# Attention kernel on one Trainium2 core: probabilities times values in three fp32r passes, and the keys' norm factor on GpSimd

## The reference

```python
q = (draft_hidden @ Wq.T).reshape(bsz, draft_len, H, HD)          # H 16, HD 128
q = _rms_norm(q, q_norm_w).transpose(0, 2, 1, 3)
kv_in = jnp.concatenate([context_hidden, draft_hidden], axis=1)   # 64 + 64 tokens
k = (kv_in @ Wk.T).reshape(bsz, total_len, KVH, HD)               # KVH 4
v = (kv_in @ Wv.T).reshape(bsz, total_len, KVH, HD).transpose(0, 2, 1, 3)
k = _rms_norm(k, k_norm_w).transpose(0, 2, 1, 3)
q = _rope(q, draft_position_ids)
k = _rope(k, full_position_ids)
scores = jnp.einsum('bhqd,bhkd->bhqk', q, k) * SCALE
probs = jax.nn.softmax(scores, axis=-1)
attn = jnp.einsum('bhqk,bhkd->bhqd', probs, v)
return attn.transpose(0, 2, 1, 3).reshape(bsz, draft_len, H * HD) @ Wo.T
```

## Time and profile before

| | |
|---|---|
| median of 3 runs | 1236.04 us (1235.15 to 1237.65) |
| span of the profiled execution | 1234.9 us |
| PE / DVE / ACT / POOL busy | 98% / 82% / 72% / 74% |
| granted TensorE clock, mean | 0.998 |
| time of the units | from 29 to about 970 us |
| expert phase | from about 970 to the end |

### The profile page before, as it was taken

The page is one execution under the profiler, slowest core; times in us unless marked ns, Lnnn a source line. Parts: engine busy times, 40 slices in busy tenths (PEclk is TensorE's granted clock), DMA queues, the critical chain, the costliest instruction groups (busy, mean ns, idle before and its releaser), DMA issues.

```text
span 1234.9 us, 31490 instructions
## 1 busy us (share of the span) xinstructions
PE 1210.5 (98%) x8781; PEld 1141.9 (92%) x8782; DVE 1008.0 (82%) x2992; ACT 885.3 (72%) x3754; POOL 919.6 (74%) x1124
## 2 busy tenths in 40 slices
PE   6899999999999999999999999999999999999998
PEld 3788999999999999999999999999999999999997
DVE  8788888888888888888888888888888677777443
ACT  7978777777777777777777777777777546666322
POOL 2678887888888888888888887888887425555654
PEclk9999999999999999999999999999999999999999
DMA  6634233322222322222333333322236536554574
GB/s 179 196 105 131 78 105 105 106 89 89 89 89 89 94 89 89 94 89 93 109 109 102 101 100 119 101 75 75 75 109 205 199 103 187 162 162 146 186 239 151
DMA packets 128792, 148.57 MB, mean 120 GB/s; under 512 B 13824, under 2 KB 108288, under 8 KB 127968
## 3 DMA queue, kind: packets, MB, share of 16 engines
q1 hardware_dynamic: 122256, 130.16, 34.8%
q0 software_dynamic: 6480, 17.77, 3.9%
HBM read 66.93 MB, written 80.76 MB: 120 GB/s over the span
## 4 chain that ended last, share of the span: by engine, by line
PE 95%; ACT 2%; DVE 2%; issue 1%; another core or an unknown queue 0%; DMA 0%; SPq 0%; DVEq 0%; ACTq 0%
PE b_kv L1711 14%; PE b_q L1697 14%; PE b_o L1795 13%; PE b_sc L1769 9%; PE b_aT L1784 9%; PE b_pT L1777 5%; PE b_qT L1758 4%; PE b_q L2031 3%; PE b_kv L2031 3%; PE b_q L1828 2%; PE b_kT L1754 2%; PE b_kT L1828 2%; PE b_aT L1946 1%; PE b_pT L2048 1%; PE b_aT L2048 1%; PE b_o L1747 1%
## 5 line engine op out<-in xcount | busy, mean ns | idle before, releaser
L1711 PE MATMUL b_kv<-w_group,kv_in_hi 128*128 128x256 f32 x992 | 205.5, 305 | 0.0
L747 POOL TENSOR_TENSOR qk_r<-qk_me,minus_half 128x6 f32<-128x6 f32 x128 | 173.7, 1357 | 10.1 <-POOL qk_me L745 0.2
L957 ACT ACTIVATE probs<-b_sc,neg_max 128x128 f32<-128x128 f32 x512 | 180.5, 373 | 0.1
L751 POOL TENSOR_TENSOR q_rot<-q_rot,q_sin 128x512 f32<-128x512 f32 x128 | 163.8, 1279 | 6.8 <-DVE q_sin L1273 1.9
L1711 PEld LDWEIGHTS b_kv<-w_group,kv_in_hi 128*128 128x128 f32 x992 | 161.8, 190 | 6.7 <-issue 0.4
L1697 PE MATMUL b_q<-w_group,kv_in_hi 128*128 128x512 f32 x496 | 164.9, 413 | 0.0
L951 ACT ACTIVATE pT<-b_pT 128x512 f32<-128x512 f32 x128 | 76.7, 599 | 102.9 <-PE b_pT L1777 100.9
L1795 PE MATMUL b_o<-wo_hi,aT_hi 128*128 128x256 f32 x480 | 143.5, 299 | 0.1
L1769 PE MATMUL b_sc<-kT,qT 128*128 128x128 f32 x1024 | 135.8, 275 | 6.2 <-ACT qT L946 4.2
L754 POOL TENSOR_TENSOR q_rot<-q_rot,qk_r 128x512 f32<-128x512 f32 x128 | 133.5, 1043 | 10.0
L1711 PE MATMUL b_kv<-w_group,kv_in_lo 128*128 128x256 f32 x496 | 139.6, 281 | 0.0
(11 more groups left out here) (309 smaller groups left out, 3949.2 us busy)
## 6 DMA issues: line engine op xcount, KB each, us to landing
xs_scratch<-zeros SPq DMA_DIRECT2D x34, 1032.0 KB, 6.2
s_in<-xs_scratch SPq DMA_DIRECT2D x71, 129.0 KB
yT_scratch<-yT SPq DMA_DIRECT2D x32, 256.0 KB
yS<-yT_scratch SPq DMA_DIRECT2D x32, 256.0 KB
routed<-ys_scratch SPq DMA_DIRECT2D x32, 256.0 KB, 3.6
w_hi_all<-w_scratch SPq DMA_DIRECT2D x3, 1536.0 KB, 14.0
x_in<-in_x SPq DMA_DIRECT2D x32, 128.0 KB, 2.3
ctx_raw<-in_ctxT SPq DMA_DIRECT2D x32, 128.0 KB, 2.6
```

The lines of the kernel that those rows point to most:

```text
L747: nc.gpsimd.tensor_tensor(qk_r[g % 2][:], qk_me[:], minus_half[:, 0:REP + NB], ALU.pow).then_inc(r_ready, 1)
L751: nc.gpsimd.tensor_tensor(q_rot[g % 2][:], q_rot[g % 2][:], q_sin[g % 2][:], ALU.add) \
L957: last = nc.scalar.activation(probs[:, j, :], b_sc[:, j * P:(j + 1) * P], ACT.Exp, bias=neg_max[g % 2][:, j:j + 1], accum_out=row_sum[g % ...
L1711: last = nc.tensor.matmul(b_kv[:, s * 2 * HD:(s + 1) * 2 * HD], kv_in[p][a][:, c, 2 * s:2 * s + 2, :], wkv_of(b, c)[:, g % KVH, :], start= ...
```

## The change

Seven things are edited; none changes what is computed beyond rounding.

1. `attend`: the values (`v_s`) and the transposed probabilities (`pT`) become high and low parts, and each of the two 256-column fp32 matmuls becomes three fp32r ones. The high parts are the ACT copies that were there; the low parts are two new DVE subtractions in each unit, `values_lo` (128x256) and `probs_lo` (128x512), both reading PSUM.
2. `turn_keys` on DVE no longer multiplies by the norm factor: four 128x128 operations become two of 128x256. POOL multiplies the sum by the factor in `key_sum`, one more 128x256 operation.
3. DVE's order: `turn_keys(n+1)` moves from behind `score_max(n)` to right behind `turn_queries(n+1)`; `values_lo(n+1)` and `probs_lo(n-1)` stand in front of `score_max(n)`.
4. The copy of kT moves from DVE to ACT, in front of the copy of qT.
5. ACT's order: the copy of the transposed probabilities comes right behind the copy of qT, the scaling of the first probability block moves from the next unit to right behind the high part of attention, in front of the squares of the queries.
6. PE's order: `probs_T(n-1)` stands in front of `scores(n)` rather than behind it and behind the small matmuls.
7. `below`, `ones`, `mask` and `seen`, the small counts of the ranks, become bfloat16. Buffers: `junk` goes (the squares are written, as fp32, to the buffers that the turn overwrites), `q_sin` and `k_sin` have one buffer in place of two, with a wait on POOL's sums.

```diff
             def key_sum(n, g):
                 need(pool, k_turned, n + 1)
-                nc.gpsimd.tensor_tensor(k_rot[g % 2][:], k_rot[g % 2][:], k_sin[g % 2][:], ALU.add) \
+                nc.gpsimd.tensor_tensor(k_rot[g % 2][:], k_rot[g % 2][:], k_sin[:], ALU.add) \
+                  .then_inc(rot_summed, 1)
+                need(pool, rot_summed, 2 * n + 2)
+                nc.gpsimd.tensor_tensor(k_rot[g % 2][:], k_rot[g % 2][:],
+                                        qk_r[g % 2][:, REP:REP + NB].unsqueeze(2).to_broadcast([P, NB, HD]), ALU.mult) \
                   .then_inc(k_ready, 1)
...
+            def keys_out(n, g):
+                need(act, kT_done, n + 1)
+                nc.scalar.activation(kT[:].rearrange("p b n -> p (b n)"), b_kT[:, 0:NB * P], ACT.Copy).then_inc(k_out, 1)
...
                     if not (end and g == 3):
                         key_squares(n + 1, g + 1)
+                        values_out(n + 1, g + 1)
...
                     if not (first and u == 0):
+                        if not (first and u == 1):
+                            keys_out(n, g)
                         queries_out(n, g)
-                    if not (end and g == 3):
-                        values_out(n + 1, g + 1)
                     if not (first and u == 0):
-                        normalize_first(n - 1, g - 1)
+                        probs_out(n - 1, g - 1)
...
-                    if not (first and u == 0):
-                        probs_out(n - 1, g - 1)
...
                     exponentials(n, g)
...
                         attended_hi(n - 1, g - 1)
+                    if not (end and g == 3):
+                        normalize_first(n, g)
                     if not (end and g >= 2):
                         query_squares(n + 2, g)
...
             def turn_keys(n, g, p):
 
-                need(dve, v_out, n + 1)
-                need(dve, r_ready, n + 1)
+                need(dve, v_hi, n + 1)
+                need(dve, rot_summed, 2 * n)
...
+            def values_lo(n, g):
+                kv = b_kv[:].rearrange("p (b w n) -> p b w n", b=NB, w=2)
+                hi, lo = v_s[g % KVH]
+                nc.vector.tensor_tensor(lo[:], kv[:, :, 1, :], hi[:].bitcast(F32), ALU.subtract).then_inc(v_lo, 1)
+
+            def probs_lo(n, g):
+                need(dve, pT_hi, n + 1)
+                nc.vector.tensor_tensor(pT[LO][:].rearrange("p b n -> p (b n)"), b_pT[:],
+                                        pT[HI][:].rearrange("p b n -> p (b n)").bitcast(F32), ALU.subtract).then_inc(pT_lo, 1)
...
                     if not (end and g == 3):
                         turn_queries(n + 1, g + 1, t + (g == 3), p1)
+                        turn_keys(n + 1, g + 1, p1)
...
+                    if not (end and g == 3):
+                        values_lo(n + 1, g + 1)
+                    if not (first and u == 0):
+                        probs_lo(n - 1, g - 1)
                     score_max(n, g)
...
-                    if not (end and g == 3):
-                        turn_keys(n + 1, g + 1, p1)
...
             def attend(n, g):
-                need(pe, v_out, n + 1)
-                need(pe, pT_out, n + 1)
+                need(pe, v_lo, n + 1)
+                need(pe, pT_lo, n + 1)
                 for s in range(NB):
-                    last = nc.tensor.matmul(b_aT[:, s * REP * S:(s + 1) * REP * S], v_s[g % KVH][:, s, :],
-                                            pT[:, s, :], start=True, stop=True)
+                    for a, b in PASSES:
+                        last = nc.tensor.matmul(b_aT[:, s * REP * S:(s + 1) * REP * S], v_s[g % KVH][a][:, s, :],
+                                                pT[b][:, s, :], start=((a, b) == PASSES[0]), stop=((a, b) == PASSES[-1]))
...
+                    if not (first and u < 1):
+                        probs_T(n - 1, g - 1)
                     scores(n, g)
...
-                    if not (first and u < 1):
-                        probs_T(n - 1, g - 1)
```

91 lines of the change are left out of this document (46 added, 45 removed).

## The result

The changed kernel takes **1388.7 us** (median of 4 runs, 1387.3 to 1389.0) against 1236.0 (1235.2 to 1237.7) for the kernel before: 1.123 times as long, 95% interval 1.121 to 1.124. Slower was forecast, but 1296 us and at most 1328. The sign and the chain held, the size did not. Its span is 1385.6 us at a granted clock of 0.997, so the clock explains nothing.

What follows compares the result with a forecast made beforehand. PE bounds the kernel before; DVE's in-order chain was to bound it after. A tile of 31.3 us for 29.29 gives 49 us over 24 tiles, plus 7 and 4: +60 on 1234.9, forecast 1296 us, range 1268 to 1328.

Steps and rivals of the forecast that it cites:

- The new chain: DVE with ACT's exponentials, one unit's first exponential to the next: 6.57 us for 5.29 before, plus work done once a tile.
- the 93 forecast: Sign on PE: its busy time from 500 to 600 us falls from 100 to about 93.
- the sum: The four units of a tile, 8.15, 7.46, 7.84 and 7.87 us, give 31.3 us for 29.29 before.
- SBUF-only terms: DVE operations priced from earlier rows: probabilities 0.65 us, x_n with the residual 0.75, normalized rows 0.54.
- may shrink by 0.6: DVE's weight piece split, 1.27 us for 440 columns, might shorten; 15 us in the lower half of the range.
- Without it the ACT path holds: 6.92.: Unit g 2 to 3 without a weight piece: ACT's path sets the length, 6.92 us instead of 7.84.
- the chain is longer: Rival, chance 0.13: fp32 squares on ACT take 0.09 us more each, 0.3 to 0.5 a unit; 1330 to 1350 us.
- What the change does on PE: `attend`: six fp32r passes take 0.69 us for 0.86, gaining 0.17 a unit, 22 us, lost while PE waits.
- PE stays the bound: Rival, chance 0.06: DVE's chain stays below PE's new unit of 7.08 us; the 22 us come in full, 1211 to 1216.
- The counts: Two bfloat16 matmuls of 8 columns a tile on PE: at most 7 us in all, taken as nothing.
- What it does on POOL: One more 128x256 multiply a unit, taken as 0.60 us, plus 0.08 for the wait, right ahead of PE's `heads_T`.
- POOL becomes the bound: Rival, chance 0.06: the multiply fills POOL's wait for ACT's squares; tile 29.1 to 30.0 us, near 1243 us.

Runs made afterwards that it cites:

- x15: Changed kernel with POOL's rotary tables cut, the two-element addition moved behind the maxima and the layer norm's x_n moved to the end of unit g 0: 1288.4 us, ratio 1.044.
- x10: Changed kernel with both low-part subtractions on DVE (values and probabilities) cut to one element, all six passes multiplying high parts: 1297.3 us, ratio 1.051.
- x1: Changed kernel with the turn of the keys on DVE put back behind the maximum of the scores: 1316.4 us, ratio 1.064.
- x5: Kernel before with only the three fp32r passes in `attend`, all on high parts, no low parts computed: 1232.3 us, ratio 0.996.
- x7: x5 with the subtraction for the weight piece moved from the end of unit g 2 to the end of g 3: 1228.1 us, ratio 0.995.
- x12: Kernel before with the bfloat16 counts alone: 1231.0 us, ratio 0.998.
- x16: Changed kernel with low-part subtractions cut to one element, and the keys' turn and two-element addition behind the maxima: 1283.4 us, ratio 1.041.

## Why the prediction was right in its sign and wrong in its size

- **"The new chain" held.** ACT starts its exponentials 0.76 to 0.78 us after the maximum starts, 0.09 or 0.10 after its end, in every unit of the tile shown; DVE waits for the exponentials 0.8 to 1.3 us in each. PE is 88% busy for the 93 forecast. x15 confirmed the sum, 30.9 us a tile for 30.6. x10 and x1 moved the time by about what stands in the chain (91 us for 93; 72 for 81), but that close agreement is luck: both also freed stalled operations and both ran into POOL's late sin table.
- **The step that failed is the pricing of its SBUF-only terms**: probabilities 0.65, x_n 0.40 (in the 0.75 for x_n with the residual), and the normalized rows, 0.54, whose two-element addition had no term. They were read where POOL did not stop them (x_n and the rows beside its power, the probabilities behind the last 0.23 us of a sum) and then used at new places, where POOL was at work. Measured they were 1.81 and 1.29 in two units of four (0.56 in the others), 0.92, and 0.48 + 1.25. The warning was in the earlier trace rows: the weight piece took 1.27 us for 440 columns where 384 took 0.65. The prediction saw it, took it into its lower half only ("may shrink by 0.6"), and didn't ask why. Another stands in the earlier trace rows: the multiply at 514.02 took 0.64 us, for the 0.56 it takes alone, because it began inside POOL's sum of 513.52. What was missed is worth some 90 us.
- **A smaller miss: "Without it the ACT path holds: 6.92."** In the five tiles without a piece the unit took 8.36 us in the changed kernel and 7.30 in x15, where the stalls were gone; there DVE waits for the sin table behind the scatter, 0.68 us in one such tile.
- **The rival "the chain is longer"** came near in time (1330 to 1350) for a wrong reason. The squares that write fp32 have a mean of 0.300 us for 0.283 (first row after, second before; groups of instructions from 300 to 900 us, busy us and then mean ns):
```profile
L944 ACT ACTIVATE q_rot<-b_q 128x128 f32<-128x128 f32 x280 | 74.4, 300 | 0.0
```
```profile
L940 ACT ACTIVATE junk<-b_q 128x128 bf16<-128x128 f32 x328 | 85.7, 283 | 0.0
```
- **"What the change does on PE"** was right for the passes: six on `b_aT` from 560.09 to 560.80, 0.71 us for 0.86.
```profile
560.09 0.28 PE L1806 MATMUL b_aT<-pT_hi,v_hi 128*128 128x256 f32 x1
...
560.68 0.28 PE L1806 MATMUL b_aT<-pT_hi,v_lo 128*128 128x256 f32 x1
```
The saving is 0.15 to 0.16 a unit; the 0.21 that the Trainium skill's page on FP8 and Floating Point Precision would give by three passes for four is not reached. That the saving is lost while PE isn't the bound was right. The rival "PE stays the bound" had priced it at 22 us; alone it brings 5 (x5), since in tiles with a weight piece DVE's stalled subtraction (x5), or what it pushes into POOL's work when it is moved (x7), takes most of the gain back. The counts, taken as nothing, bring 3.3 us where PE is the bound (x12), below their ceiling of 7.
- **"What it does on POOL"**: the multiply takes 0.61 for the 0.60 taken. That it doesn't matter was right only behind the longer chain. Once the chain is shortened (x1, x16), POOL's queue bounds the unit with the sin table, at 1283 us in x16 and not at the 1243 of the rival "POOL becomes the bound", which had no price for one late table a tile.
- **Where the 153 us are.** They don't add up by parts: 72 in x1 (order), 91 in x10 (low parts), 100 in x15 (contention), each taken from the changed kernel. Each cure uncovers the next wait, and the first two also take stalls away, so neither number is the price of its own cause alone.

## What to carry to other kernels

Before an operation is moved along an in-order engine, look at what the other engine does at the new time. On VectorE a multiply, addition or scaling that has its inputs and its output in SBUF, however small, may stand until GpSimd's operation is over, as here beside its sums, multiplies and tables, though not beside its power on six columns; what reads PSUM did not here. A duration in a trace that is too long for its size (1.35 us for 440 columns beside 0.64 for 384) was such a stand-still here, and the operation should be priced without it and with it wherever it may fall. A stalled operation counts as busy, so a high busy share is not yet work. And count the low parts of a split operand as chain time on the engine that makes them: 0.94 us a unit of DVE work was paid here to save PE 0.16.
